# A decoder layer on one core: mask rows, first value projection, cross-attention fills and feed-forward copies put in another order

## Time and profile before

| | us |
|---|---|
| median of 3 runs | 2219.49 (2218.57 to 2231.32) |
| the profiled execution, own time | 2217.53 |
| its span in the trace | 2215.5 |
| PE busy | 2105.6 (95%) |
| DVE busy | 1559.6 (70%) |
| ACT busy | 803.9 (36%) |
| POOL busy | 762.4 (34%) |

### The profile page before, as it was taken

One profiled execution on the slowest core, in us unless ns is written; L12 is line 12 of the kernel. 1 busy time (PEld: TensorE's weight loads), 2 busy tenths in 40 slices (PEclk: granted clock), 3 DMA queues, 4 the chain that ended last, 5 costly groups with the idle time before them and its releaser, 6 DMA issues. The chain is left out here.

```text
span 2215.5 us, 35363 instructions
## 1 busy us (share of the span) xinstructions
PE 2105.6 (95%) x11638; PEld 1499.3 (68%) x11638; DVE 1559.6 (70%) x2829; ACT 803.9 (36%) x1843; POOL 762.4 (34%) x532
## 2 busy tenths in 40 slices
PE   5899999999999999999999999889999999699998
PEld 4677787887887778878878878643333333278776
DVE  7657887887887556878878888568888887432221
ACT  1223233233233232332332332317667766652221
POOL 3234344344343343443443433321222221221211
PEclk9999999999999999999999999989999999999999
DMA  6121011011111220110101110474566654311110
GB/s 214 38 95 56 8 54 44 24 54 30 38 54 36 77 106 2 55 45 24 54 32 37 54 34 4 82 153 90 104 118 119 119 103 92 113 38 58 58 38 20
DMA packets 60484, 142.36 MB, mean 64 GB/s; under 512 B 10942, under 2 KB 25478, under 8 KB 55398
## 3 DMA queue, kind: packets, MB, share of 16 engines
q1 hardware_dynamic: 57622, 138.65, 24.0%
q10 hardware_dynamic: 2768, 2.51, 0.5%
HBM read 93.47 MB, written 17.54 MB: 50 GB/s over the span
## 5 line engine op out<-in xcount | busy, mean ns | idle before, releaser
L1712 DVE TENSOR_REDUCE x_mx<-x_pm 128x1 f32<-128x512 f32 x512 | 324.0, 683 | 58.3 <-PE x_pm L1814 57.5
L1553 ACT ACTIVATE x_E<-x_pd 128x512 f32<-128x512 f32 x497 | 266.7, 602 | 117.9 <-PE x_pd L1833 116.9
L1140 PE MATMUL a_pj<-a_wvg_h,q_big 128*128 128x512 f32 x1024 | 287.0, 408 | 4.2 <-DVE a_rm L800 4.2
L1124 PE MATMUL a_pj<-q_big,a_wqk_h 128*128 128x512 f32 x1024 | 290.1, 405 | 0.4 <-POOL a_wqk_l L632 0.4
L1140 PEld LDWEIGHTS a_pj<-a_wvg_h,q_big 128*128 128x128 f32 x1024 | 186.1, 189 | 54.1 <-issue 4.8
L1124 PEld LDWEIGHTS a_pj<-q_big,a_wqk_h 128*128 128x128 f32 x1024 | 183.1, 188 | 40.0 <-POOL a_wqk_l L632 1.3
L800 DVE TENSOR_TENSOR a_rm<-a_pj,a_rope 128x1024 f32<-128x1024 f32 x128 | 155.5, 1216 | 74.1 <-PE a_pj L1124 72.8
L519 ACT ACTIVATE a_v<-a_pj 128x256 f32<-128x256 f32 x128 | 49.1, 384 | 420.3 <-PE a_pj L1140 420.3
L670 POOL TENSOR_TENSOR a_ogl<-a_ogf,a_ogh 128x512 fp32r<-128x512 f32 x62 | 82.2, 1347 | 282.0 <-ACT a_ogf L558 282.0
L892 DVE TENSOR_TENSOR a_acc<-a_po,a_acc 128x512 f32<-128x512 f32 x128 | 85.9, 687 | 88.3 <-PE a_po L1253 88.3
L1847 PE MATMUL x_pa<-x_E,x_vx 128*32 128x512 f32 x1024 | 140.7, 612 | 1.0 <-ACT x_raw L1567 1.0
(11 more groups left out here) (228 smaller groups left out, 4503.9 us busy)
## 6 DMA issues: line engine op xcount, KB each, us to landing
a_qk_raw<-in_wqk SPq DMA_DIRECT2D x16, 1024.0 KB, 5.4
a_vg_raw<-in_wvg SPq DMA_DIRECT2D x16, 1024.0 KB, 4.9
a_wo_raw<-in_wo SPq DMA_DIRECT2D x16, 512.0 KB, 3.6
x_Q<-x_hi SPq DMA_DIRECT2D x20, 256.0 KB
x_K<-x_hi SPq DMA_DIRECT2D x20, 256.0 KB
a_acc<-in_w SPq DMA_DIRECT2D x6, 704.0 KB, 4.3
a_wt<-in_w SPq DMA_DIRECT2D x24, 176.0 KB, 2.3
weights_scratch<-a_wt SPq DMA_DIRECT2D x24, 176.0 KB, 1.9
```

What stands on the lines that cost most here:

```text
L1124: last = mm(pj[:, j % 2, :], wa[:, c, j * P:(j + 1) * P], xa[:, c, p * UT:(p + 1) * UT], start=k == 0, stop=k == 11)
L1140: last = mm(pj[:, tt % 2, :], xa[:, c, t0:t0 + P], wa[:, c, :], start=k == 0, stop=k == 11)
L1553: nc.scalar.activation(E[:, n % ESLOTS, :], dot_bank(n), ACT.Exp, scale=XD ** -0.5).then_inc(exp_done, 1)
L1712: nc.vector.reduce_max(mx[:, u % 2, at:at + 1], pm[:, k % 3, :], AX_X).then_inc(pm_done, 1)
```

## The change

Five things are changed; no operation on the data is added or dropped.

1. `mask_products` on DVE is now only the five operations that need nothing but the mask, and stands at the very start, before `variances(0)`. The three high copies are made by ACT (`mask_highs`), between `high_qk(0)` and unit 0; two subtractions (`mask_lows`) stand on DVE after `low_x(0)`; the last three products are made by ACT after that.
2. In unit 0, PE does vg(1) before scores(0), vg(2) before scores(1).
3. In unit 0, DVE does gate products 1 and 2 ahead of the pairs of `a_evac`.
4. `LATE` is one step earlier: the pieces of Q go in steps G = 0 to 5, no longer 1 to 6.
5. At the start of feed-forward DVE takes pieces 3 to 6 in turn with the four statistics, where it took 0 to 4, then did all statistics and the root's input, then took 5 and 6.

The semaphores `rows_h` and `rows_l` are new. The diff without the lists of their names:

```diff
@@ -383,6 +383,7 @@
             load_qk(1, 1)
             load_vg(1, 1)
             sp.wait_ge(rows_b, 6)
+            sp.wait_ge(rows_l, 2)
             for i, line in enumerate(mq + mk):
                 sp.dma_start(rows_dram[:, i, :], line).then_inc(rows_out, 16)
             for i in range(2, 6):
@@ -519,6 +520,16 @@
                 nc.scalar.activation(v[:, p, tt, :], pj[:, tt % 2, 0:256], ACT.Copy).then_inc(v_done, 1)
                 nc.scalar.activation(gs[:, p, tt, :], pj[:, tt % 2, 256:512], ACT.Tanh, scale=0.5).then_inc(g_tanh, 1)
 
+            def mask_highs():
+
+                act.wait_ge(rows_a, 2)
+                for row, src in ((0, ra), (2, rb), (3, rb)):
+                    nc.scalar.activation(mq[row].bitcast(F32R), src, ACT.Copy).then_inc(rows_h, 1)
+                act.wait_ge(rows_h, 3)
+                act.wait_ge(rows_l, 1)
+                for row, src in ((2, 0), (3, 1), (4, 0)):
+                    nc.scalar.activation(mk[row].bitcast(F32R), mq[src], ACT.Copy, scale=-4.0).then_inc(rows_b, 1)
+
             def turned_ok(m):
                 if isinstance(m, int) and m == 0:
                     act.wait_ge(rows_out, 16 * 11)
@@ -609,6 +620,7 @@
             nc.scalar.activation(ws1_h[:], ws1r[:], ACT.Copy).then_inc(ws1_hi, 1)
             high_x(0)
             high_qk(0)
+            mask_highs()
             units(act.Fori, unit, core)
 
         @block.gpsimd
@@ -717,30 +729,21 @@
 
         @block.vector
         def _(dve):
-            def mask_products(part):
+            def mask_products():
 
                 V = nc.vector
-                high = [line.bitcast(F32R) for line in mq]
-                if part == 1:
-                    dve.wait_ge(rows_a, 2)
-                    V.tensor_copy(high[0], ra).then_inc(rows_a, 1)
-                    V.tensor_copy(high[2], rb).then_inc(rows_a, 1)
-                    V.tensor_copy(high[3], rb).then_inc(rows_a, 1)
-                    return
-                if part == 2:
-                    dve.wait_ge(rows_a, 5)
-                    V.tensor_tensor(high[1], ra, mq[0], ALU.subtract).then_inc(rows_a, 1)
-                    V.tensor_tensor(high[4], rb, mq[2], ALU.subtract).then_inc(rows_a, 1)
-                    dve.wait_ge(rows_a, 7)
-                    for row, src in ((2, 0), (3, 1), (4, 0)):
-                        V.tensor_scalar(mk[row].bitcast(F32R), mq[src], -4.0, None, ALU.mult).then_inc(rows_b, 1)
-                    return
                 dve.wait_ge(m_in, 16)
                 V.tensor_scalar(ra, m8, -NEG_ROOT, NEG_ROOT, ALU.mult, ALU.add).then_inc(rows_a, 1)
                 V.tensor_scalar(rb, m8, NEG_ROOT, None, ALU.mult).then_inc(rows_a, 1)
                 for i in range(2):
                     V.tensor_scalar(mk[i].bitcast(F32R), m8, 0.0, -4.0 * NEG_ROOT, ALU.mult, ALU.add).then_inc(rows_b, 1)
                 V.tensor_scalar(mk[5].bitcast(F32R), m8, 0.0, 1.0, ALU.mult, ALU.add).then_inc(rows_b, 1)
+
+            def mask_lows():
+
+                dve.wait_ge(rows_h, 3)
+                nc.vector.tensor_tensor(mq[1].bitcast(F32R), ra, mq[0], ALU.subtract).then_inc(rows_l, 1)
+                nc.vector.tensor_tensor(mq[4].bitcast(F32R), rb, mq[2], ALU.subtract).then_inc(rows_l, 1)
 
             def variances(k):
                 if k == 4:
@@ -961,16 +964,12 @@
                 rotate(n, 0)
                 if scaled(n):
                     clip(n, p)
-                if isinstance(n, int) and n == 0:
-                    mask_products(0)
                 if began(n, 2):
                     add_out(l, p, (0, 1))
                 nf4(n, p, k0, 0)
                 if began(n, 1):
                     ok_chain(m, pm)
                 rotate(n, 1)
-                if isinstance(n, int) and n == 0:
-                    mask_products(1)
                 if began(n, 1):
                     ok_sum(m)
                 if began(n, 2):
@@ -983,8 +982,6 @@
                 if final(n):
                     variances(4)
                 rotate(n, 2)
-                if isinstance(n, int) and n == 0:
-                    mask_products(2)
                 nf4(n, p, k0, 2)
                 if isinstance(n, int) and n < 2:
                     scalers((3 * n, 3 * n + 1))
@@ -1004,11 +1001,15 @@
                 inverse_sums(n, p)
                 if began(n, 1):
                     mean_squares(m)
+                if not began(n, 1):
+                    gate_product(n, p, 1)
                 a_evac(n, 0)
                 a_evac(n, 1)
                 if began(n, 1):
                     gated(m, pm)
-                gate_product(n, p, 1)
+                    gate_product(n, p, 1)
+                else:
+                    gate_product(n, p, 2)
                 a_evac(n, 2)
                 a_evac(n, 3)
                 nf4(n, p, k0, 4)
@@ -1018,7 +1019,8 @@
                     normalised(4)
                 if isinstance(n, int) and n == 1:
                     inverse_scalers()
-                gate_product(n, p, 2)
+                if began(n, 1):
+                    gate_product(n, p, 2)
                 nf4(n, p, k0, 5)
                 gate_product(n, p, 3)
                 if prepared(n):
@@ -1046,9 +1048,11 @@
                 normalised(5)
                 add_out(m, pm, range(4))
 
+            mask_products()
             variances(0)
             normalised(0)
             low_x(0)
+            mask_lows()
             scores_in(0)
             def scales_loaded(half):
                 if half == 0:
@@ -1289,10 +1293,16 @@
                 if began(n, 1):
                     outputs(m, pm, 0)
                     outputs(m, pm, 1)
-                scores(n, 0)
-                project_vg(n, g, p, 1)
-                scores(n, 1)
-                project_vg(n, g, p, 2)
+                if began(n, 1):
+                    scores(n, 0)
+                    project_vg(n, g, p, 1)
+                    scores(n, 1)
+                    project_vg(n, g, p, 2)
+                else:
+                    project_vg(n, g, p, 1)
+                    scores(n, 0)
+                    project_vg(n, g, p, 2)
+                    scores(n, 1)
                 project_vg(n, g, p, 3)
                 if prepared(n):
                     transposes_x(PREPS[n + 1], n + 1, (0, 1))
@@ -1446,7 +1456,7 @@
         block = s.enter_context(nc.Block())
 
         FILLS = {9: ((1, 0),), 10: ((1, 1),), 11: ((1, 4),), 12: ((1, 5),), 13: ((1, 2),), 14: ((1, 3),)}
-        LATE = {k + 1: ((0, k),) for k in range(6)}
+        LATE = {k: ((0, k),) for k in range(6)}
         FIRST = tuple((0, k) for k in range(6))
         SECOND = {0: ((1, 0),), 1: ((1, 1),), 2: ((1, 4), (1, 5)), 3: ((1, 2), (1, 3))}
 
@@ -2032,16 +2042,20 @@
         def _(dve):
             V = nc.vector
 
+            def take(r):
+                dve.wait_ge(w12_ready, 2 * r + 2)
+                V.tensor_copy(w2[:, :, r * P:(r + 1) * P], spread(turned(1, r))).then_inc(taken_dve, 1)
+
             def norm_stats(g):
                 first = isinstance(g, int) and g == 0
-                if first:
-                    dve.wait_ge(x_first, 16)
-                else:
+                if not first:
                     dve.wait_ge(x_in, 16 * g + 16)
                     dve.wait_ge(rstd_done, g)
                 for tt in range(4):
-                    if first and tt == 2:
-                        dve.wait_ge(x_in, 16)
+                    if first:
+                        if tt % 2 == 0:
+                            dve.wait_ge((x_first, x_in)[tt // 2], 16)
+                        take(BY_DVE - 4 + tt)
                     V.bn_stats(stats[:, tt, :], xt[:, tt, :]).then_inc(stat, 1)
                 dve.wait_ge(stat, 4 * g + 4)
 
@@ -2097,15 +2111,9 @@
                 for tt in range(1, 4):
                     add(g, tt)
 
-            def take(r):
-                dve.wait_ge(w12_ready, 2 * r + 2)
-                V.tensor_copy(w2[:, :, r * P:(r + 1) * P], spread(turned(1, r))).then_inc(taken_dve, 1)
-
-            for r in range(BY_DVE - 2):
+            for r in range(BY_DVE - 4):
                 take(r)
             norm_stats(0)
-            for r in range(BY_DVE - 2, BY_DVE):
-                take(r)
             normed(0, 0)
             normed(0, 1)
             low(0, 0)
```

More of the change, by code:

```diff
@@ L275, in self_attention @@
             "raw_0 raw_1 scaler_done part_done summed inv_done scale_step flat_out flat_in deq_out deq_loaded "
-            "x_first ident_in_done const_late m_in rows_a rows_b rows_out cross_in next_in kept_in cross_w "
+            "x_first ident_in_done const_late m_in rows_a rows_h rows_l rows_b rows_out cross_in next_in kept_in cross_w "
             "cp_ready cp_done chi_done clo_done stack_0 wt_0 wt_1 nf4_step nf4_stored")
```

2 lines of the change are left out of this document (1 added, 1 removed).

## The result

| | before | changed |
|---|---|---|
| median of 20 runs each, us | 2224.48 (2216.95 to 2238.91) | 2237.89 (2227.09 to 2247.36) |
| ratio to before | | 1.0057 (95% interval 1.0041 to 1.0072) |
| profiled execution, span | 2215.5 | 2227.0 |

The change makes the kernel slower by 0.57%, about 13 us. Forecast was 4.4 us faster, with a range of 2207 to 2226. The median of before was 5.0 us higher in these 20 runs than in the three shown first, so against the same runs the forecast is off by about 18 us (+13.4 for -4.4).

A forecast was written before the change was run, and what follows sets the result against it. PE, busy 95% of the span, was taken as the bound, so changes count through its idle stretches. Terms 0.5 - 8.5 + 7.3 - 5.3 + 1.6 = -4.4 us gave 2215.1 us for the median, range 2207 to 2226.

The forecast's parts named there:

- The start: Kernel start: five mask operations on DVE ahead of the first statistics may delay them; +0.5 us (0 to 2.0).
- Unit 0: Self-attention's first unit: rotate(3) 5.2 us earlier, vg(1) fills 2.6 us of PE's wait, clock 0.7; -8.5 us (-5.5 to -10.3).
- Pieces of Q: Cross-attention, G = 8: the last piece lands earlier, so waits there and batch 6's clock loss shrink; -5.3 us (-2 to -5.8).
- Feed-forward: Start of feed-forward: copies ahead of the root's input leave DVE's wait empty, first normalised tokens later; +1.6 us (1.3 to 2.2).
- The context: Cross-attention, batches 1 to 5: a piece of Q ahead delays the context load by 1.5 us; +7.3 us (+2.4 to +14.5).
- main term: The context's delay in cross-attention; called wrong if waits at G = 4 grow by less than 1 or more than 2 us.
- The first rival: Cross-attention: one queue's transfers served in order, context lands 2.3 us later; +14.5 for +7.3, total +2.8 us; chance 0.20.

The follow-up runs named there:

- e8: Kernel before with only the new unit 0 order (vg ahead of scores on PE, gate products earlier on DVE); profiled span 2233.0 us for 2215.5.
- e3: Changed kernel with the context load issued ahead of the piece of Q in step G = 0; ratio to the kernel before 0.9931.
- e5: Changed kernel with the context load ahead of the piece of Q and also of the results of the group before; ratio to the kernel before 0.9920.
- e12: Kernel before with the new feed-forward order on DVE alone; ratio to the kernel before 1.0018.
- e9: Changed kernel with the context load ahead of the results at G = 0 and the feed-forward part undone; ratio to the kernel before 0.9892.
- e13: e9 with the pieces of Q back in steps G = 1 to 6; ratio to the kernel before 0.9931.
- e4: Changed kernel with one piece of Q ahead of the context load and none behind it until G = 4; profiled span 2264.7 us.

## Why the prediction was wrong

- **The start**, +0.5: the first statistics came 0.36 us later. The number fits by luck: the tokens ended the wait, not the mask operations. With the mask operations first the statistics begin at 4.64 to 4.98 us (11 executions), without them at 4.50 to 4.92 (4), so no cost is to be seen.
- **Unit 0**, -8.5: -8.35 at the next transposes, and -8.7 without the start. Right in size and in the steps: rotate(2) at 33.80 for 33 to 34, rotate(3) at 41.28, a wait of 0.98 ahead of vg(0). The split was right too, 5.16 for masks (5.2 forecast) and 2.36 for the projection (2.6 forecast). Together they give 0.83 more than their sum; 0.42 of that is that e8's first tokens came late. The gain lasted: self-attention ends at 1442.0 to 1447.0 in the ten executions with both parts and at 1451.3 to 1454.5 in the three with neither. Two small things were missed. The first subtraction takes 3.58 us, not about 0.7, beside `low_qk` on POOL, and POOL's `low_vg` came at 26.23. Both were hidden as forecast.
- **Pieces of Q**, -5.3: -2.7 in the second stretches and -3.75 in that of batch 6, together -6.5, beyond the bound of -5.8 (which is itself 0.3 more than its rows give, 3.9 + 1.6). The reason given holds in batch 6 (the wait at G = 8 falls from 2.41 to 0.17 us). Of the -2.7 a part is not the pieces: PE came to G = 8 late, after its wait at G = 4. In e3 and e5, where it does not, the second stretches give -0.7 and -1.3, and with batch 6 the term is -4.6 and -5.0: right.
- **Feed-forward**, +1.6: the mechanism is there (1.20 us of idle time on DVE, first tokens 1.2 later), the cost is not: 0 in this pair. The first projection comes 2.0 us later after the load, but runs at full clock; before, the clock was 0.59 of full from 1946 to 1948, and its second half took 1.91 us where it now takes 1.08. The two rows of before and of the changed kernel are below. After the first four groups of products 0.35 us of the 2.0 is left (they end 21.6 and 21.9 us after the load). That the clock gives it back is what this pair shows; e12 leaves up to 9 us open, so it is not shown in general.
- **The context, +7.3, is the step that failed.** It was +25.5 us. "I take 1.5" for how much later the load lands is what went wrong, and so is the upper end, "256 KB at the 109 GB/s ... = 2.3 us". The issue came 0.6 us later as forecast, and the landing 3.1 us after that later still, 3.7 in all. The grid shows what each ingredient is worth. A piece at full rate is not the ceiling of what a piece costs a load behind it. The row I leaned on, batch 0 (5.7 us), has no `x_sums` load ahead of it and its later pieces begin 1.5 us after it: two differences, of which I named one and weighed neither.
- **The size of the slack and of the clock** made it worse. Waits at G = 4 grew by 1.05, 3.87, 3.76, 4.95 and 3.45 us, 17.1 in all, where the mark for a wrong main term was "more than 2". Batch 1, whose load had landed late already (9.7 us), is the 1.05. The other 8.4 of the 25.5 us go with the half clock behind waits of 4 us: 2.3 us each in batches 2 to 4, 1.6 in batch 5, none in batch 1, which had its wait before too. I had added 1.0 for two batches.

PE's timeline of before, then of the changed kernel, where the first projection of feed-forward begins:

```profile
1945.44 1.28 PE L2173 MATMUL f_pa<-q_big,f_w 128*128 128x512 f32 x4 [1.50 <-DVE f_xl L2066]
1946.52 1.91 PE L2173 MATMUL f_pa<-f_xl,f_w 128*128 128x512 f32 x4
```

```profile
1958.89 1.16 PE L2181 MATMUL f_pa<-q_big,f_w 128*128 128x512 f32 x4 [1.51 <-DVE f_xl L2080]
...
1959.89 1.08 PE L2181 MATMUL f_pa<-f_xl,f_w 128*128 128x512 f32 x4
```

The first rival, the context waiting for a full piece, had the mechanism and the sign, but also too small a price (+14.5 for +25.5), and I gave it 0.20. The landings of 4.4, 7.5 and 9.5 us with none, one and two pieces ahead bear out that order counts. The Trainium skill, "DMA: Bandwidth & Descriptors", section "Queues, rings and completion order", has each DMA engine take descriptors in ring order; these landings agree with it. The 7.0 us with three pieces behind against 4.4 with none are a cost that ring order by itself gives no reason for. The measurement decides.

A reservation on single executions: from SP's first load of cross-attention to batch 1 the 15 profiled executions took 93 to 102 us, so the +2.3 us there in the table can't be put down to the change.

## What to carry to other kernels

- Put the load with the least slack first on its queue, before stores and before loads that only have to be early; here moving it alone made 0.9931 (e3) of 1.0057. Only then is bringing the others forward a gain (0.9892 in e9 for 0.9931 in e13). Issued ahead of a wait for stores as well (e5), it caused no wait at all; the ratio, 0.9920, is too near that of e3 to tell them apart.
- When a load is moved behind another, its cost is not the other's bytes over the rate: look for the same load with and without company, and where the trace has none, take the bound from the worst landing seen (9.7 us here, and even that is under the 10.1 that came), not from the calmest.
- A wait can cost more than its length through the clock. In the first stretches, e4's waits of 1.4 to 1.8 us cost no more than themselves, e3's 2.18 us made its stretch 3.1 us longer and the changed kernel's 4.51, in place of 0.64, 6.2. So count each wait's own size, not only their sum.
